# Cross-attention and feed-forward kernel: maxima of the first output in two pieces, and turned pieces read ahead of VectorE's additions

## What is computed

```python
q = _w8a8_linear(layernorm(x), wq, bq); k = cond @ wk.T + bk; v = cond @ wv.T + bv
scores = einsum('bhnd,bhld->bhnl', q, k) / sqrt(32) + mask
o = einsum('bhnl,bhld->bhnd', softmax(scores), v)
s = max(max(abs(o), axis=-1) / 127, 1e-8)      # largest value of each row of the output
x = x + (clip(round(o / s)) @ quantised(wo).T) * scales + bo
x = x + down(silu(gate(layernorm(x))) * up(layernorm(x)))
```

## Time and profile before

| what | us |
|---|---|
| median of 3 runs (lowest, highest) | 477.38 (476.62, 478.38) |
| the profiled execution: own time, span of its profile | 477.79, 476.0 |
| TensorE busy | 465.8 |
| VectorE busy | 365.0 |
| ScalarE busy | 261.9 |
| GpSimd busy | 238.5 |

### The profile page before, as it was taken

How to read it: one execution, slowest core, us unless ns; L and a number is a source line. 1 busy time by engine, 2 the same in 40 slices (tenths; PEclk the granted TensorE clock), 3 DMA queues, 4 the chain that set the end, 5 groups by cost and what they waited for, 6 DMA issues and landing times.

```text
span 476.0 us, 6950 instructions
## 1 busy us (share of the span) xinstructions
PE 465.8 (98%) x2390; PEld 302.0 (63%) x2390; DVE 365.0 (77%) x486; ACT 261.9 (55%) x465; POOL 238.5 (50%) x131
## 2 busy tenths in 40 slices
PE   8999899999999999999999999999999999999996
PEld 5888588677654454545454454534468778888885
DVE  3589888897988798978879898789966468574325
ACT  3586987321567576666756796667824223222220
POOL 3004211912489888787978878787022122222230
PEclk9999999999999999999999999999999999999999
DMA  5999997998677928091642800030244424446322
GB/s 181 319 313 393 372 280 283 303 275 329 139 197 163 298 72 178 2 211 33 139 106 64 181 2 1 1 133 2 67 154 134 134 78 155 157 133 229 132 68 91
DMA packets 44390, 77.41 MB, mean 163 GB/s; under 512 B 5281, under 2 KB 13505, under 8 KB 44353
## 3 DMA queue, kind: packets, MB, share of 16 engines
q1 hardware_dynamic: 44064, 76.41, 54.3%
q10 hardware_dynamic: 288, 0.52, 0.3%
HBM read 57.95 MB, written 18.87 MB: 161 GB/s over the span
## 4 chain that ended last, share of the span: by engine, by line
PE 77%; DVE 13%; DMA 4%; ACT 3%; issue 2%; SPq 0%; DVEq 0%; ACTq 0%
PE ps L881 13%; PE ps L903 12%; PE ps L853 12%; PE ps L778 8%; PE ps L779 8%; PE ps L990 4%; PE ps L991 4%; PE ps L802 3%; DVE neg_m L1444 3%; PE ps L690 2%; PE ps L692 2%; PE ps L691 2%; DMA raw<-in_ctx_t 2%; PE ps L813 2%; DVE kq_lo L1418 1%
## 5 line engine op out<-in xcount | busy, mean ns | idle before, releaser
L1444 DVE TENSOR_REDUCE neg_m<-ps 128x1 f32<-128x1024 f32 x128 | 149.7, 1216 | 23.4 <-PE ps L853 23.4
L1193 ACT ACTIVATE p_t<-ps 128x512 f32<-128x512 f32 x256 | 137.6, 597 | 43.9 <-PE ps L881 40.4
L1777 POOL TENSOR_TENSOR p_sum<-p_sum,p_t 128x1024 f32<-128x1024 f32 x44 | 105.5, 2410 | 3.2 <-ACT p_t L1193 0.8
L881 PE MATMUL ps<-q_st,k_st 97*128 97x512 f32 x256 | 93.5, 425 | 1.0 <-ACT p_t L1193 0.9
L1777 POOL TENSOR_TENSOR p_sum<-p_t 128x1024 f32<-128x1024 f32 x29 | 70.1, 2419 | 30.0 <-ACT p_t L1193 16.3
L853 PE MATMUL ps<-k_st,q_st 96*128 96x512 f32 x256 | 83.3, 407 | 0.8 <-DVE neg_m L1444 0.4
L881 PEld LDWEIGHTS ps<-q_st,k_st 97*128 97x128 f32 x256 | 47.5, 188 | 51.2 <-ACT p_t L1193 37.3
L778 PE MATMUL ps<-xt_hi,k_st 128*128 128x512 f32 x176 | 68.9, 391 | 0.0
L779 PE MATMUL ps<-xt_lo,k_st 128*128 128x512 f32 x176 | 68.6, 390 | 0.0
L903 PE MATMUL ps<-p_t,v_gr 128*32 128x512 f32 x512 | 68.2, 604 | 0.1
L1721 POOL TENSOR_TENSOR v_st<-v_st,bv_bc 128x512 f32<-128x512 f32 x16 | 20.1, 1286 | 88.8 <-DVE qin L1389 35.0
(11 more groups left out here) (143 smaller groups left out, 664.0 us busy)
## 6 DMA issues: line engine op xcount, KB each, us to landing
k_st<-k_hi_d SPq DMA_DIRECT2D x16, 512.0 KB, 6.9
mask_sb<-in_mask SPq DMA_DIRECT2D x3, 2048.0 KB, 13.2
w_int<-in_w_gate SPq DMA_DIRECT2D x22, 256.0 KB, 2.6
w_int<-in_w_up SPq DMA_DIRECT2D x22, 256.0 KB, 2.9
w_int<-in_w_down SPq DMA_DIRECT2D x22, 256.0 KB, 3.6
k_hi_d<-kq_hi SPq DMA_DIRECT2D x16, 256.0 KB, 6.7
k_lo_d<-kq_lo SPq DMA_DIRECT2D x16, 256.0 KB, 7.4
v_d<-v_st SPq DMA_DIRECT2D x16, 256.0 KB, 10.9
```

Of the source, the lines that this page charges most:

```text
L881: mm = pe.matmul(ps[:, bank, :], k_st[g % SLOTS][0:rows, j, P * lc:P * lc + P], q_st[g % SLOTS][0:rows, j, :], start=True, stop=not with_mask)
L1193: act.activation(p_t[:, q % 4, j, :], ps[:, score_bank(q, j), :], ACT.Exp).then_inc(exp_done, 1)
L1444: dve.tensor_reduce(neg_m[:, g % 2, nt, j:j + 1], ps[:, bank:bank + 2, :], AX_XY, ALU.max, negate=True).then_inc(max_read, 1)
L1777: pool.tensor_tensor(total, former, p_t[:, q % 4, hs, :], ALU.add).then_inc(added_pool, 1)
```

## The change

Two things are changed, both in what VectorE does and when. First, the largest values of sequence 0's output: instead of four reductions of 512 columns after all of the output is there, two reductions take the first 384 columns (two tiles each, 768 elements a partition, in steps (4, 2) and (4, 4)), one takes the last 128 columns of all four tiles (512 elements, in (4, 6)), and a small operation joins them. Second, where a step has a piece of the tail and an addition of VectorE, VectorE handles the piece first. That is so in (6, 1), (6, 5), (7, 3) and (7, 4).

```diff
@@ -85,6 +85,7 @@
         rs = sb("rs", [P, B, NT], F32)
         rt = sb("rt", [P, B, NT], F32)
         qmx = sb("qmx", [P, 6, NT], F32)
+        qmx_parts = sb("qmx_parts", [P, 2, NT], F32)
         qsc = sb("qsc", [P, 6, NT], F32)
         qin = sb("qin", [P, 6, NT], F32)
         eps_c = sb("eps_c", [P, 1], F32)
@@ -363,7 +364,8 @@
             PLACES.insert(PLACES.index(("tile", before)), ("tail", kind, j))
         place = {key: p for p, key in enumerate(PLACES)}
 
-        LARGEST_AT = {(OT, 5): 0, (OT, 6): 1, (OT, 7): 2, (OT + 1, 0): 3}
+        LARGEST_AT = {(OT, 2): (0, 1), (OT, 4): (2, 3)}
+        LARGEST_OVER = (OT, 6)
         SCALE_LC = 2
         SCALE_AFTER, ROUND_AFTER = {2: (0, 1, 2, 3)}, 3
         STATISTICS_AFTER, NORMALISE_AFTER = 7, 8
@@ -1366,9 +1368,21 @@
                 then(dve.tensor_reduce(qmx[:, s, :], src, AX_X, ALU.max, apply_absolute_value=True))
                 steps_from_largest(s)
 
-            def largest_of_output(t):
-                dve.tensor_reduce(qmx[:, O_SET, t:t + 1], o_sb[:, t, :], AX_X, ALU.max,
+            def largest_of_former_groups(tiles):
+
+                dve.wait_ge(o_done, OT - 1)
+                rows = slice(tiles[0], tiles[-1] + 1)
+                dve.tensor_reduce(qmx_parts[:, 0, rows], o_sb[:, rows, 0:C - P], AX_X, ALU.max,
                                   apply_absolute_value=True).then_inc(o_largest, 1)
+
+            def largest_of_output():
+
+                dve.wait_ge(o_done, OT)
+                then(dve.tensor_reduce(qmx_parts[:, 1, :], o_sb[:, 0:NT, C - P:C], AX_X, ALU.max,
+                                       apply_absolute_value=True))
+                dve.wait_ge(o_largest, len(LARGEST_AT))
+                dve.tensor_tensor(qmx[:, O_SET, :], qmx_parts[:, 0, :], qmx_parts[:, 1, :],
+                                  ALU.max).then_inc(o_largest, 1)
 
             def inverse_steps_of_output():
                 dve.wait_ge(o_steps, 1)
@@ -1603,16 +1617,16 @@
                     maxima(units)
                     if turned:
                         normalise_output(g - 1)
-                    if quad(g, lc) >= 2:
-                        add(quad(g, lc) - 2)
                     for key in tail:
                         for k, bank in enumerate(ring_banks(key)):
                             tail_part(0, key[1], key[2] + k, bank)
+                    if quad(g, lc) >= 2:
+                        add(quad(g, lc) - 2)
 
                     if (g, lc) in LARGEST_AT:
-
-                        dve.wait_ge(o_done, OT)
-                        largest_of_output(LARGEST_AT[g, lc])
+                        largest_of_former_groups(LARGEST_AT[g, lc])
+                    elif (g, lc) == LARGEST_OVER:
+                        largest_of_output()
                     elif (g, lc) == (OT + 1, 1):
                         inverse_steps_of_output()
                     elif (g, lc) == (G - 2, LC - 1):
@@ -1752,7 +1766,7 @@
             for q in range(G * LC):
                 if q == LC * (OT + 1) + 1:
 
-                    pool.wait_ge(o_largest, NT)
+                    pool.wait_ge(o_largest, len(LARGEST_AT) + 1)
                     pool.tensor_scalar(qsc[:, O_SET, :], qmx[:, O_SET, :], 1.0 / QMAX, QUANT_EPS,
                                        ALU.mult, ALU.max).then_inc(o_steps, 1)
                 if q == 2 * SET + 1:
```

## The result

The changed kernel takes 489.08 us (median of 6 runs, 488.05 to 491.08), the kernel before 477.13 (6 runs, 476.37 to 478.38): a ratio of 1.0263, 95% interval 1.0242 to 1.0284, so 12 us slower. The profiled execution took 491.08 with a span of 489.3, which is 13.3 more than the span before. Of that, 1.23 lie ahead of everything that was changed: the sums of (4, 2) start at 240.05 instead of 238.82.

What follows compares the result with a forecast made beforehand. TensorE, busy 465.8 of 476.0 us, was taken to bound the kernel; the terms 0.5 + 1.3 - 0.7 + 5.8 + 2.4 = +9.3 us gave 486.9 us, range 477 to 490, the forecast's own 484 to 489.

Steps and rivals of the forecast that it cites:

- the likeliest case: The forecast itself: the five terms' sum without a fall of TensorE's clock, 484 to 489 us, chance 0.45.
- rival 3: TensorE's 5.8 us wait lets its clock fall from 2.4 to 1.2 GHz: 489 to 492 us, chance 0.13.
- Term 1: Steps (4, 2) to (4, 6): longer reductions delay VectorE's maxima and TensorE's units that need them, +0.5 us.
- Term 2: Step (4, 6): the joining operation waits for a GpSimd addition, delaying the maxima of (4, 7), +1.3 us.
- Term 3: Step (6, 1): O copies ahead of the addition to quad 47 remove the wait before the sums, -0.7 us.
- Term 4: Addition to quad 51 behind (6, 5)'s residuals: GpSimd runs late, holds the root's small steps, delays the sums, +5.8 us.
- Term 5: Step (7, 3): N pieces ahead of the addition to quad 57 delay it and the exponential of quad 60, +2.4 us.
- rival 1: Small steps with two SBUF inputs aren't held by GpSimd: sum +3.9, 481.5 us; with mixtures 478.9 to 484, chance 0.22.
- rival 2: VectorE keeps its turn and runs the whole root before GpSimd's next addition: 476 to 478.9 us, chance 0.15.

Runs made afterwards that it cites:

- W first: Kernel before, with only the W pieces put ahead of VectorE's addition to quad 51 in (6, 5): 486.36 us, ratio 1.0207.
- the reductions alone: Changed kernel with the old order of additions ahead of tail pieces, so only the reductions of the largest values differ from before: ratio 1.0059.
- the other joining operation: Only the reductions changed, old order kept, the two pieces joined by a one-input reduction instead of a two-input operation: ratio 1.0031.
- N first: Kernel before, with only the N pieces put ahead of the additions to quads 57 and 58: 480.25 us, ratio 1.0098.
- GpSimd not held back: Kernel before with W pieces ahead in (6, 5), GpSimd's second half of quad 53 no longer waiting for the addition to quad 51: ratio 1.0047.

## Why the prediction came out as it did

The direction, the places and the mechanism of the waits were right; the time was 2.2 us too low, because the likeliest case left out the fall of the clock that rival 3 had. The 489.08 lies just beyond the forecast's own 484 to 489, in what rival 3 was given. That it came so near is in part luck: the missing clock, 3.5, was made up for by terms that were 0.9 too large and by adding them to 477.6 where the kernel before measured 477.13.

- **Term 1**, +0.5: measured +0.48 with the joining operation taken out. TensorE's row at 254.23 waited for the second maximum behind the longer reduction, the unit that was named; counted from the sums it came 1.01 late, as worked out.
- **Term 2**, +1.3: measured 1.24, as the difference of the two joining operations. It was held for most of one GpSimd addition, not a whole one.
- **Term 3**, -0.7: measured -0.70, both in the whole change and alone.
- **Term 4**, +5.8: the second half of the sums started 332.62 - 327.53 = 5.09 late (in W first alone 330.62 - 325.49 = 5.13). The chain was as predicted (the residuals wait for TensorE, the addition is late, GpSimd is late, the root meets it), and the experiments with GpSimd released or held back show each end of it. Two details were wrong. I took it that GpSimd gets an addition in between any two small steps. A step that starts ahead of GpSimd's next addition slips through: one at 323.11, where GpSimd's next starts at 323.19, and three from 327.94, in a rest of 0.45. The step at 325.62 stands behind a start of GpSimd's at 325.52 and is held. And the rest itself, between two additions of GpSimd of which the second waits for the first, was not in my working, though the timeline of POOL before has it at the same addition, in a row that the earlier trace rows leaves out (shown below this list). Behind the rest came a fourth long step. The two nearly cancel; the term was 0.7 too large.
- **Term 5**, +2.4: measured 2.32 alone. The suspicion that the exponential had waited for VectorE's addition, not for TensorE as the row names it, was right: twice it came 0.08 to 0.09 behind the end of the moved addition.
- **The sum**: the five measured terms make 0.48 + 1.24 - 0.70 + 5.09 + 2.32 = 8.4, and 9.3 was predicted. The trace has 11.95. Nearly all of the missing 3.5 is the clock by the traces: with TensorE busy through the long wait the stretch took 23.93 instead of 27.21, 3.3 less (by the medians less came back, as said above). W first alone lost 2.4 to the clock and has one fall of it; the whole change has a second, in (7, 3). The step that failed is the choice of "the clock stays at 1.00" for the likeliest case. Its price had been put at 4 at most and was about 3.3 in the profiled executions, 2.4 under W first alone; with 3.3 and the terms as predicted the forecast would have been 490.2.
- **The rivals**: the small two-input steps are held (2.27 and 2.29 for 0.16), so rival 1 falls; VectorE doesn't keep its turn (four long steps), so rival 2 falls; rival 3 happened beside the forecast's own terms.
- **The Trainium skill** (SBUF — State Buffer, "Who interferes with whom") has VectorE instructions with two SBUF inputs excluded by a reading GpSimd for a whole instruction, and tensor_reduce free of it. The joining operation shows both, 2.04 as the one form and 0.16 as the other. The Trainium skill's rule on the clock (TensorE: Matmul & The Clock Gate, "What's actually happening"), that an idle TensorE has its clock halved and gets it back by working, agrees with the stretches shown: 0.50 from 330 to 336, behind the idle 4.99, and full again from about 336.6, where TensorE had been at work since 332.62. I should have given it more weight than 0.13.

The row of POOL before that term 4 speaks of:

```profile
326.01 2.53 POOL L1777 TENSOR_TENSOR p_sum<-p_sum,p_t 128x1024 f32<-128x1024 f32 x1 [0.45 <-POOL p_sum L1777]
```

What stays open: the medians of several kernels stand further from the kernel before than the marks in their traces do: the reductions alone +3.0 beside +1.72, with the other joining operation +1.4 beside +0.48, W first +10.3 beside +7.64, N first +4.2 beside +2.32, GpSimd not held back +2.2 beside +0.94. By the marks the four parts add up to 11.0, the whole change has 11.95; by the medians they add up to 17.0. The profiled executions were among the faster ones of these kernels, and no wait in them accounts for it. So the shares of the terms are those of the traces; the medians bear out their signs and order.

## What to carry to other kernels

Moving an instruction on one engine moves what waits for it on another, and so where the two next meet: an addition moved behind two residuals (four short operations, and their wait for TensorE) made TensorE wait 5 us, none of it where it was moved, by bringing GpSimd's long instructions beside a chain of short dependent ones. Count on it that some steps of such a chain wait for a whole instruction of the other engine each (here three of nine, and the step ahead of them for most of one), unless a dependency keeps that engine at rest, and give such a small step the form of a reduction where that is possible. TensorE's wait of 5 us cost more than itself here, since the clock fell: look at the granted clock behind each long wait.

## What the runs showed that was not expected

- Four elements, two inputs: 0.16 alone, 2.04 to 2.35 beside GpSimd; the same joining as a reduction 0.16 beside GpSimd.
- The clock fell inside the wait of 4.99, and stayed at 1.2 GHz for 3.9 us of work behind it.
- A wait of 2.35 in (7, 3) left the clock at 1.00 in the one traced execution of N first; five others of the same kernel had a mean clock of 0.993 to 0.996.
- A GpSimd addition that waits for the one ahead of it left a rest of 0.45, and three small steps of VectorE ran there; the kernel before has the same rest.
